# Two steps of scores, then two steps of value products, in the first cross attention of a decoder kernel

## The reference

```python
att = jnp.einsum('bhqd,bhkd->bhqk', q, k) * scale
att = jnp.where(causal[None, None], att, -jnp.inf)
y = jnp.einsum('bhqk,bhkd->bhqd', jax.nn.softmax(att, axis=-1), v)
attc = jnp.einsum('bhqd,bhkd->bhqk', qc, kc) * scale
y = y + jnp.einsum('bhqk,bhkd->bhqd', jax.nn.softmax(attc, axis=-1), vc)
y = y.transpose(0, 2, 1, 3).reshape(x.shape[0], T, C)
return y @ Wp + bp
```

## Time and profile before

| | us |
|---|---|
| three runs, median | 717.5 (lowest 714.95, highest 976.4) |
| the profiled execution | 714.63 |
| its span, from the first instruction to the last | 712.6 |
| the stretch of the steps with halves at full clock | 93 to 358.5 in the span |
| the last 22 steps, without halves | 358.5 to 389 |

### The profile page before, as it was taken

One profiled execution on the slowest core, in us unless ns is written; L12 is line 12 of the kernel. 1 busy time (PEld: TensorE's weight loads), 2 busy tenths in 40 slices (PEclk: granted clock), 3 DMA queues, 4 the chain that ended last, 5 costly groups with the idle time before them and its releaser, 6 DMA issues. The chain is left out here.

```text
span 712.6 us, 13577 instructions
## 1 busy us (share of the span) xinstructions
PE 617.4 (87%) x5175; PEld 337.9 (47%) x5175; DVE 522.9 (73%) x698; ACT 444.3 (62%) x801; POOL 223.9 (31%) x284
## 2 busy tenths in 40 slices
PE   8989899999999999999999778996447789969996
PEld 5645433333333333433333457883123456637884
DVE  5369889999999999999924557995596467746432
ACT  3556578888888888888886434565842145644223
POOL 7224522353555577666620110000000460005000
PEclk9999989999999999999999898999769889989999
DMA  8259576545565554444100394440000400000000
GB/s 204 91 149 282 189 205 172 141 96 151 141 154 158 137 115 96 95 115 96 43 19 1 110 367 145 149 147 0 0 1 0 162 1 1 1 1 0 1 1 29
DMA packets 43261, 70.67 MB, mean 99 GB/s; under 512 B 12476, under 2 KB 31636, under 8 KB 42688
## 3 DMA queue, kind: packets, MB, share of 16 engines
q1 hardware_dynamic: 31696, 38.34, 20.5%
q0 software_dynamic: 10896, 29.25, 13.0%
q10 hardware_dynamic: 608, 2.25, 1.5%
HBM read 44.35 MB, written 24.79 MB: 97 GB/s over the span
## 5 line engine op out<-in xcount | busy, mean ns | idle before, releaser
L962 ACT ACTIVATE prob<-ps 128x512 f32<-128x512 f32 (+2 forms) x480 | 253.1, 582 | 46.1 <-PE ps L738 39.0
L1083 DVE TENSOR_REDUCE pm<-ps 128x2 f32<-128x1024 f32 x192 | 226.0, 1216 | 6.7 <-PE ps L700 4.9
L761 PE MATMUL ps<-prob,vst 128*9 128x256 f32 (+1 forms) x1664 | 129.8, 384 | 10.2 <-ACT o_all L950 10.2
L738 PE MATMUL ps<-qq,kc 50*128 50x256 bf16 (+1 forms) x832 | 134.3, 275 | 0.2
L700 PE MATMUL ps<-kc,qq 48*128 48x512 bf16 x384 | 116.3, 388 | 2.9 <-DVE pm L1083 2.6
L738 PEld LDWEIGHTS ps<-qq,kc 50*128 50x128 bf16 (+1 forms) x832 | 52.2, 96 | 94.2 <-ACT prob L962 69.3
L761 PEld LDWEIGHTS ps<-prob,vst 128*9 128x9 f32 (+1 forms) x1664 | 25.1, 88 | 51.7 <-ACT prob L962 39.1
L1801 POOL DMA_DIRECT2D w_w<-in_w x2 | 1.1, 536 | 140.8 <-SPq L1797 140.8
L1090 DVE TENSOR_REDUCE nm<-ps 128x4 f32<-128x512 f32 (+1 forms) x32 | 30.6, 958 | 14.9 <-PE ps L688 14.9
L700 PEld LDWEIGHTS ps<-kc,qq 48*128 48x128 bf16 x384 | 32.9, 93 | 13.3 <-DVE pm L1083 9.4
L688 PE MATMUL ps<-masks_b 64*128 64x256 bf16 x256 | 37.6, 269 | 0.0
(11 more groups left out here) (362 smaller groups left out, 1309.2 us busy)
## 6 DMA issues: line engine op xcount, KB each, us to landing
kc<-kc_scr SPq DMA_DIRECT2D x32, 300.2 KB, 5.0
comb_bc<-comb_scr SPq DMA_DIRECT2D x7, 512.0 KB, 4.4
below<-rden_scr POOLq DMA_DIRECT2D x13, 256.0 KB, 6.5
ctx<-ctx_scr POOLq DMA_DIRECT2D x1, 3204.0 KB, 15.8
raw<-in_wexp POOLq DMA_DIRECT2D x8, 384.0 KB, 3.7
exp_scr<-raw_high POOLq DMA_DIRECT2D x8, 384.0 KB, 3.2
exp_scr<-raw_low POOLq DMA_DIRECT2D x8, 384.0 KB, 4.3
kc_scr<-hi SPq DMA_DIRECT2D x6, 400.2 KB, 4.8
```

The lines of the kernel that those rows point to most:

```text
L738: last = pe.matmul(bank[0:p, j * TQ:(j + 1) * TQ], kc[s][rows, j, t * 128:t * 128 + p], qq[s][rows, 0, j, :], start=(j == 0), stop=True, s ...
L761: last = pe.matmul(o_ps[32 * hh:32 * hh + VW, kind * TQ + q0:(kind + 1) * TQ], value[:, hh * VW:(hh + 1) * VW], prob[0:k, (NST * n + t) % ...
L962: act.activation(prob[0:p, g % P_RING, 2 * e:2 * e + 2, q0:TQ], s2[0:p, k % S2_RING, 0:2 * w].rearrange("p (i q) -> p i q", i=2), ACT.Exp, ...
L1083: dve.tensor_reduce(pm[:, m % 2, c, :, jt], banks, AX.X, ALU.max).then_inc(s1_read, 1)
```

## The change

PE gives out the scores and halves of two steps, then the value products of two steps. The products of a unit's first step, where they would come second of a pair, are left for the next pair, which then has three; the pair before has one. ACT copies a unit's outputs after the exponential (t = 1, e = n % 2): in odd units where it did, in even units one exponential earlier.

```diff
@@ -835,11 +835,15 @@
+                    given = 0
                     for g in range(NU * NST):
                         n, t = g // NST, g % NST
                         scores_and_half(g, g + HALVES + S1_LEAD)
-                        if g >= 2:
-                            outputs((g - 2) // NST, (g - 2) % NST)
+                        if g % 2:
+                            upto = g - 2 if (g - 2) % NST == 0 else g - 1
+                            for i in range(given, upto):
+                                outputs(i // NST, i % NST)
+                            given = max(given, upto)
...
-                    for t in (NST - 2, NST - 1):
-                        outputs(NU - 1, t)
+                    for i in range(given, NU * NST):
+                        outputs(i // NST, i % NST)
...
-                            if t == 1 and e == 1 and n:
+                            if t == 1 and e == n % 2 and n:
                                 copy_out(n - 1)
```

## The result

The changed kernel takes 743.7 us (median of four runs, 741.3 to 745.4) against 716.2 before: a ratio of 1.041, interval 1.038 to 1.044. The ratio leaves out the disturbed run of 976.4 us, which the median 716.2 still counts, so it isn't quite the quotient of the two medians. The profiled execution took 741.3, its span is 739.3, against 714.6 and 712.6.

The account below looks back on a forecast made before the run. PE, with DVE and ACT nearly full, set ordinary steps before; afterwards the PE, ACT, PE loop would. Units +25.1 and last 22 steps +1.5 sum to +27 on 714.6, 741 to 742; plus three, 743 us, range 720 to 757.

Parts of the forecast that it names:

- The wait in the ring: Three score banks: a pair's last scores wait for its first exponential, start at 1.15 us, not 0.66; pair 2.44 us.
- The copy: ACT's copy of a unit's outputs delays exponentials; pairs (0,1) and (2,3) of even units take 5.26 us, two plain pairs 4.88.
- The turn: Where a unit's maxima turn on PE: even pair (8,9) takes 3.44 us, odd pair (7,8) 3.66 us.
- The sum: Even unit 21.24 and odd 19.61 us, together 40.85; 20.4 a unit against 18.67, +25.1 us over 14.2 units.
- The last 22 steps: 358.5 to 389 us, no maxima: about 32 us against 30.5, +1.5, PE's extra products partly filling the wait.
- A: The crossings win: last scores at 0.66 us, DVE bounds, unit 17.3 to 17.5 us, 697 us total; chance 0.08.
- The price of a crossing: Each switch on PE between scores and value products costs 0.12 us; the change removes two a pair.
- B: Copy and turn hide in PE's waits and DVE's vanished backlog: unit 19.2 us, total 725; chance 0.15.
- C: PE's waits halve the granted clock for one 6.8 us stretch in each unit: +34 us, 776; chance 0.06.
- the prediction's loop: PE, ACT, PE within a pair: 1.15, 0.31, 0.43 and 0.55 sum to 2.44 us, the new bound.

Follow-up runs that it names:

- the light old order: Kernel before with a fourth score bank (maxima of e = 1 left out) and DVE's wide reductions over half their elements: 701.6 us, ratio 0.979.
- the light new one: Changed kernel with a fourth score bank (maxima of e = 1 left out) and DVE's wide reductions over half their elements: 697.7 us, ratio 0.975.

## Why the prediction was right

**The wait in the ring** was the step that decided, and it held: last scores 1.14 after the pair's start (worked out 1.15), pair 2.45 (2.44), and with a fourth bank the run was back at the time of before. It could be read before the change since the old order has one place a unit where two score blocks stand closer than usual, behind the short products of step 14.

**The copy.** The pairs that hold it took, in the unit that begins at 209.17:

```profile
209.17 0.09 PEld L738 LDWEIGHTS ps<-qq,kc 50*128 50x128 bf16 x1 [0.43 <-issue]
...
211.41 0.09 PEld L738 LDWEIGHTS ps<-qq,kc 50*128 50x128 bf16 x1 [0.22 <-ACT prob L966]
...
212.68 0.09 PEld L738 LDWEIGHTS ps<-qq,kc 50*128 50x128 bf16 x1 [0.94 <-ACT prob L966]
213.17 0.09 PEld L738 LDWEIGHTS ps<-qq,kc 50*128 50x128 bf16 x1 [0.38 <-ACT prob L966]
...
214.48 0.09 PEld L738 LDWEIGHTS ps<-qq,kc 50*128 50x128 bf16 x1 [0.43 <-ACT prob L966]
```

5.31 for pairs (0,1) and (2,3), worked out 5.26; first bank of S(3) at 3.51, last scores at 4.00 (3.51 and 3.97).

**The turn.** Pair (8,9) starts 219.71, PE's half behind reduction 0 comes 1.93 later (worked out 1.92), the next pair at 3.45 (3.44):

```profile
219.71 0.09 PEld L738 LDWEIGHTS ps<-qq,kc 50*128 50x128 bf16 x1 [0.43 <-ACT prob L966]
...
221.64 0.09 PEld L700 LDWEIGHTS ps<-kc,qq 48*128 48x128 bf16 x1 [0.90 <-DVE pm L1087]
...
223.16 0.09 PEld L738 LDWEIGHTS ps<-qq,kc 50*128 50x128 bf16 x1 [0.43 <-ACT prob L966]
```

In the odd unit pair (7,8) runs from 197.82 to 201.48, 3.66 as worked out.

**The sum.** Two units took 41.16, worked out 40.85. The 0.3 missing is small terms taken too low, the largest the pair with masked step 13 in even units (2.67 for 2.55). From the first copy to step 218 the profiled execution lost 26.7 us. The forecast had 25.1 for 14.2 units (its own lengths give 1.76 a unit and 24.9, not 1.77); at 1.91 a unit the 13.4 units of this stretch make 25.6, and a stretch of 3.4 us at half clock at 359 us accounts for the rest: the unit that holds it took 21.32 us, 1.2 more than its like. The last 22 steps cost 0.4 more than before, not 1.5. That PE's extra products fill the waits better than I allowed is likely, but wasn't tried. The first copy came 0.4 later, and everything behind the last copy took 0.7 less. So 27 in the sum against 26.7 in the spans is partly luck: units taken 0.16 too short, the last steps 1.1 too long.

**The rivals.** A fell because its condition (last scores before 1.04) was not met: they came at 1.14. The price of a crossing that it rests on did hold. When a bank was added to meet it, its time of 697 didn't come either: with its wait gone, the new order ran at 18.83 a unit, not DVE's 17.3 to 17.5, with PE waiting 17.1 us for reductions in 140 (110 to 250 us) and DVE busy 127 of them, not throughout. My reading is that the copy and the turn cost PE and DVE time that the other can't use; that wasn't tried apart. That step of the rival, going straight to the least possible DVE time, was wrong. B fell with the copy and turn pairs, which did not hide in the waits: a unit took 20.58, not 19.2. C: the clock stayed at full over the two units shown. It was at half for one stretch of 3.4 us between the first copy and the last 22 steps, which cost 1.2 us, not for one in each unit.

## What to carry to other kernels

Before batching work on one engine to save its switches, count the buffers that the batch fills against the ring they come from. One more than the ring holds puts the consumer's whole latency (here 0.50 to the start of the exponential, 0.59 for it, 0.06 back) into every batch, however idle that consumer is on average; a saving of 0.24 a pair became a loss of 0.27. And try the parts of a change apart: here the small edit, which costs 0.4 us in every two units in the new order, gains 0.45% in the old one, and 0.9% when it is made in every unit.

## What was not expected of the hardware

Nothing of a single instruction. What surprised me is how exactly the stretch repeats: with the two lengths of the prediction's loop taken from one unit, pairs came out within 0.02 us of their working in most places. And a transfer that was late by 0.6 us at most in the kernel before (the maxima's rows, 100 to 340 us) held PE up for as long as 2.9 us in the light old order and 4.7 in the light new one, though SP issued it at once in the unit shown; from within the wait of 4.7 on, the granted clock was at half for 13.7 us.
